# A three-stage decoder layer on one core: 16 instead of 50 matmuls over ones ahead of the set-up

## What is computed

```
x = layernorm(x + self_attention(x))                 # one head, weights Wq Wk Wv Wo, biases
x = layernorm(x + cross_attention(x, ctx, ctx))      # 16 heads of 64, weights W_Q W_K W_V W_O
x = layernorm(x + expert_ffn(x))                     # 8 experts
# expert_ffn: scores = softmax(x @ Wr); each expert takes its 1024 best tokens of 4096,
# gelu(X @ W1 + b1) @ W2 + b2, times the score, added back to those tokens
```

## Time and profile before

| | us |
|---|---|
| median of 3 runs | 674.19 (673.83 to 674.24) |
| the profiled execution | 674.73 |
| its span, first to last instruction | 672.8 |

### The profile page before, as it was taken

The page is one execution under the profiler, slowest core; times in us unless marked ns, Lnnn a source line. Parts: engine busy times, 40 slices in busy tenths (PEclk is TensorE's granted clock), DMA queues, the critical chain, the costliest instruction groups (busy, mean ns, idle before and its releaser), DMA issues.

```text
span 672.8 us, 11862 instructions
## 1 busy us (share of the span) xinstructions
PE 565.0 (84%) x3914; PEld 473.0 (70%) x3914; DVE 431.4 (64%) x1007; ACT 317.3 (47%) x721; POOL 277.0 (41%) x313
## 2 busy tenths in 40 slices
PE   9989999999999999999999979621399999896700
PEld 9978898889889989988988968400167775565600
DVE  1337578567766766775785776588965686424576
ACT  1577557666755755765675552100043333331105
POOL 7202233223223222322332332100577777777766
PEclk9999999999999999999999989755589999988765
DMA  5002202302211320221142020480122455534662
GB/s 184 1 27 78 95 2 88 96 0 86 95 47 39 95 86 1 94 86 54 41 148 70 1 71 9 160 230 0 36 57 79 152 179 178 159 112 142 211 232 110
DMA packets 50547, 61.09 MB, mean 91 GB/s; under 512 B 10578, under 2 KB 36435, under 8 KB 50260
## 3 DMA queue, kind: packets, MB, share of 16 engines
q1 hardware_dynamic: 45984, 52.00, 23.8%
q0 software_dynamic: 4096, 8.66, 4.6%
q10 hardware_dynamic: 436, 0.03, 0.0%
HBM read 35.37 MB, written 25.30 MB: 90 GB/s over the span
## 4 chain that ended last, share of the span: by engine, by line
PE 46%; DVE 25%; issue 12%; POOL 8%; ACT 6%; DMA 2%; DVEq 0%; POOLq 0%; ACTq 0%
PE PS L1238 10%; PE PS L1459 6%; PE PS L1477 6%; PE PS L1264 6%; PE PS L1246 6%; DVE csum L895 3%; POOL spread L612 3%; PE PS L1182 3%; DVE pc L889 3%; DVE above L1013 3%; POOL shared L602 2%; DVE cmax L884 2%; PE PS L1255 2%; ACT VOeven L673 2%; ACT pc L693 2%
## 5 line engine op out<-in xcount | busy, mean ns | idle before, releaser
L577 POOL TENSOR_TENSOR pn<-pc,crcp 128x1232 f32<-128x1232 f32 x32 | 72.0, 2252 | 180.2 <-DVE crcp L898 180.2
L602 POOL DMA_INDIRECT shared<-table,idx x64 | 63.4, 991 | 66.2 <-DVE idx L1077 47.6
L1238 PE MATMUL PS<-cT_hi,heads_hi 128*128 128x308 f32 x256 | 83.7, 327 | 1.1 <-DVE shared L945 0.6
L673 ACT ACTIVATE shared<-PS 128x308 f32<-128x308 f32 (+1 forms) x144 | 62.0, 471 | 42.1 <-PE PS L1273 29.8
L1238 PE MATMUL PS<-cT_hi,heads_lo 128*128 128x308 f32 x256 | 78.0, 305 | 0.0
L1238 PE MATMUL PS<-cT_lo,heads_hi 128*128 128x308 f32 x256 | 77.5, 303 | 0.0
L1246 PE MATMUL PS<-shared,x1T 128*128 128x512 f32 (+1 forms) x192 | 72.4, 513 | 4.4 <-DVE pc L889 4.0
L612 POOL DMA_INDIRECT spread<-pn,idx x64 | 66.4, 1037 | 19.5 <-issue 18.0
L808 ACT ACTIVATE shared<-PS,b1T 128x512 f32<-128x512 f32 x64 | 44.0, 687 | 56.3 <-PE PS L1459 56.3
L895 DVE TENSOR_REDUCE csum<-pc 128x16 f32<-128x1232 f32 x32 | 45.8, 1430 | 33.7 <-ACT pc L693 33.7
L1477 PEld LDWEIGHTS PS<-w,shared 128*128 128x128 f32 x512 | 64.1, 205 | 4.1 <-issue 3.8
(11 more groups left out here) (173 smaller groups left out, 1148.1 us busy)
## 6 DMA issues: line engine op xcount, KB each, us to landing
spread<-zeros SPq DMA_DIRECT2D x128, 128.0 KB, 2.1
VOT<-spread SPq DMA_DIRECT2D x64, 256.0 KB, 5.1
xboth<-in_x SPq DMA_DIRECT2D x16, 256.0 KB, 2.8
w<-in_W SPq DMA_DIRECT2D x2, 2048.0 KB, 10.5
table<-x SPq DMA_DIRECT2D x16, 128.0 KB, 1.9
fin<-table SPq DMA_DIRECT2D x1, 2048.0 KB, 19.1
out_x<-fin SPq DMA_DIRECT2D x8, 256.0 KB, 2.0
cin<-in_ctx SPq DMA_DIRECT2D x8, 154.0 KB, 2.5
```

What stands on the lines that cost most here:

```text
L577: pool.tensor_tensor(pn[:, e, 0:HK].rearrange("p (h k) -> p h k", h=HEADS), pc[:, e, :].rearrange("p (h k) -> p h k", h=HEADS), crcp[:, e, ...
L602: pool.indirect_dma_start(xg[:, e % 3, h, :], None, table, bass.IndirectOffsetOnAxis(ap=idx[:, e, h:h + 1], axis=0)).then_inc(gathered[e % ...
L673: act.activation(dst, src, ACT.Copy).then_inc(free[bank_of(at, name)], 1)
L1238: i = pe.matmul(bank[:, 0:4 * KEYS], w[a][:, h, :], cT[b][:, :], start=(n == 0), stop=(n == 2))
```

## The change

Only one number differs. The constant gives how many matmuls over ones stand ahead of the set-up.

```diff
-WARM = {"first": 50, "products": 20}
+WARM = {"first": 16, "products": 20}
```

## The result

The changed kernel took 666.64 us in the median of 4 runs (665.11 to 668.38), the kernel before 674.22 (673.83 to 674.24): 7.58 us less, ratio 0.989 with a 95% interval of 0.9864 to 0.9916. Forecast were 666.6 us and a gain of 7.63. No run of the four lies within 1.2 us of 666.6: the forecast fell between the pairs. In the lower pair the granted clock of the whole run is 0.920 and in the upper 0.918. So two things need an explanation: the 7.6, and the 3 us that lie between equal runs.

What follows compares the result with a forecast made beforehand. The front was taken as a straight line on PE, which works there without a gap. The median before, 674.19 us, less 68 records (7.63 us), gave 666.56, forecast 666.6; range for 8 in 10: 664.8 to 668.5 us.

Steps and rivals of the forecast that it cites:

- the removed records: PE's front, ones ahead of the set-up: 68 records go, all at the fast clock, 0.1122 us each, 7.63 us.
- The total, 666.6: Whole kernel: median before of 674.19 us less 7.63 gives 666.56, forecast as 666.6 us, chance 0.88.
- The loads: Weight loads at the front don't move; W_O lands at 5.6 us, 1.9 us ahead of the set-up, so no wait.
- POOL's ladder: POOL's constants at the front end at 22.20 us, 1.76 us before the addition of biases is released; costs nothing.
- The clock's rise: PE's front: a later rise stretches the remaining 32 records equally in both kernels, so no gain or loss is taken.
- second rival: Front: clock rises only in the second set of ones, set-up runs slow; +5.0 us, 671.6 us, chance 0.04.
- The later steps of the clock: From the attention's end on, clock changes may shift against the work; valued at zero, about 2 us either side, usually less.
- its three places: Attention's end (397 to 399 us), first expert's first layer (1.95 us lost), a second layer near the end (2.3 us lost).
- Code fetch in the loop: Rival: PE's moved loop code is fetched on each of 6 passes, 1.2 us a stop; 673.8 to 681 us, chance 0.03.

Runs made afterwards that it cites:

- the second trace with 16: Trace from rerunning the changed kernel unaltered (16 matmuls ahead of the set-up, 20 behind); that execution took 668.8 us, the rerun's median 667.90 us against 674.77 before.
- the unfilled traces: Traces of kernels without 15 extra matmuls over ones in PE's 3.71 us attention wait; adding them to the changed kernel measured 666.56 us against 667.65.
- the slow series: Series trying 10 matmuls behind the set-up, matmuls in the attention's wait, or both, against the kernel before; every kernel took some 40 us longer, before 718.50 us.

## Why the prediction was right, step by step

**That the removed records were fast, at 0.112 us each.** Right. The front's shift is 7.63 and a part that goes with the time of the clock's rise; where the rise fell on the same record with 50 and with 16, the shift was 7.54. 33 in place of 50 and 10 in place of 20 fit the same pitch, the latter at 0.112 us between traces whose set-ups start within 0.01 us of each other.

**The total, 666.6.** The mechanism is right, but that the median came out at 666.64 is luck: it stands between two pairs 2.6 us apart. In the two later series in which the totals can be read the same change was worth 6.87 and 6.24 us, 0.8 and 1.4 less than forecast. What took the rest is open. Two of the three traces of the changed kernel lost 1.4 and 2.2 us at the attention's end and the one trace of before lost none, but one trace of before doesn't tell whether the removal makes that loss more frequent.

**The loads.** Right that there is no wait with 16, and with 8 a wait for W_O until 5.58, at the 5.6 us that the issue and the landing gave. The 1.9 us of cover were too many: the load took between 4.3 and 4.9 us from trace to trace, and when the clock rose at 4.3 us 0.4 and 0.3 us of cover were left.

**POOL's ladder.** Right that it costs nothing; the cover is 0.93 us in the trace and not 1.76, since PE was 1.11 us sooner and the ladder ended 0.27 sooner. With 10 behind the set-up it is gone, and the addition (line 572) starts at 21.92, right behind the ladder's last step, with no loss seen: from the first to the last heads matmul it is 354.15 us there and 354.19 in the trace with 20.

**The clock's rise, "no gain or loss".** Wrong as a view of one execution. The first record under 421 ns started between 4.3 and 7.0 us in the twelve traces that begin with ones, and with it the rest of the program moves: with 16 the set-up started at 6.41 us at the earliest and at 7.77 at the latest. For the mean it holds within what the traces can tell: 7.29 us over the nine traces with 16 and 15.20 over the two with 50, 7.9 apart. The Trainium skill says on its page "TensorE: Matmul & The Clock Gate", Part 1, that the count of slow matmuls changes from run to run with the same kernel; here it was 14 records in one trace of the changed kernel and 26 in another, so the runs agree. Its other half, that the warm-up is a matter of time and not of a count, these runs do not settle: with 8 and with none 46 and 48 records were slow instead of 14 to 27, but the time from the first matmul to the rise was longer as well, 8.9 and 8.6 us instead of 3.1 to 5.9.

**The set-up doesn't bring the clock up (second rival).** With 16 this never came into play, the rise lay inside the 32 records in every trace. Its price was 5.0 us by rows; with none the slow set-up and second set took 2.3 and 1.8 us more, 4.1 together, of which 2.34 were left at the first heads matmul against the second trace with 16, since PE had started the set-up sooner. Whether the 64-row set-up matmuls can bring the clock up is not settled: with 8 it rose in the last but one of them, at 10.1 us; with none all 32 ran slow and the rise came behind them, at 14.6 us, 3.6 us into the ones. With 8 there was an idle time of 0.67 us as well, and one trace of each doesn't tell what the set-up did from where the moment fell.

**The later steps of the clock, zero within 2 us.** The size was right, and one of its three places too (the end of the attention, up to 2.2 us); the first layer of the first expert stayed slow in all of the unfilled traces (5.3 to 5.8 us for its first eight matmuls, the slow series left out), and from the search to the end these took 239.2 to 240.5 us. But "less in most runs", taken from three runs within 0.41 us, was wrong: 11 runs of the kernel before spread over 2.2 us in each of two series, and the changed kernel over 2.6 to 4. The stated range of 664.8 to 668.5 held the four runs of the result, the prediction's own 665 to 668.2 only three of them, and neither held the later single ones, up to 669.86; the medians of the later series, 667.90 and 667.65, lie inside both.

**Code fetch in the loop.** Did not happen: no packet of an instruction queue from 120 to 355 us.

## What to carry to other kernels

- A stream that only keeps an engine busy costs its pitch, start to start, as long as nothing else would have filled the time. Read from the records which of them ran at the slow clock: those that a cut removes from the end are the fast, cheap ones, and cutting into the slow ones gave nothing here (8 in place of 16: 668.04 and 667.90 us), because the work behind them ran at the slow clock instead.
- How many such matmuls are wanted here is set by the later of two times: when the loads land (5.5 to 6.1 us), and when the clock is up (4.3 to 7.0 us, changing from execution to execution). Beyond that, each is a loss of its pitch.
- Three runs that agree within 0.4 us don't bound the scatter of a kernel whose clock steps; compare landmarks in the traces (the first and last record of a line) before reading a difference of 1 or 2 us between medians.

## What the hardware showed that was not expected

- The moment at which the clock rises, for the same code from the same start at 1.13 us, was 4.3 us in two traces, 5.3 and 5.6 in two, and between 6.4 and 7.0 in eight; what sets it is not seen in the profile.
- In each of the nine traces in which PE stands idle for 3.71 us near the attention's end the granted clock falls behind it and stays down over work that follows. What that costs hangs on which work it is: nothing to be seen when it is the transposes, 1.4 us when it is the first group of line 1264.
- In one series the experts' stage was 36 to 42 us longer in every trace (from the first line 1459 record to the end 227.2 us in the trace with 10, 185.6 in the trace of before). PE stood idle there between matmuls of one group with no releaser in the profile (28.8 us in 34 places ahead of line 1441, up to 1.9 us each). The cause is open.
